# First attention: the key mask added by GpSimd to the shifted relative scores, in place of four mask products of TensorE a tile

## The chip, the core and the metric

The kernel runs on one core of a Trainium2 chip. Its engines work side by side and meet by semaphores: TensorE (PE, with its weight loads PEld), VectorE (DVE), ScalarE (ACT), GpSimd (POOL) and the Sync queue (SP), which here only issues transfers. The metric is the device time of one execution, in microseconds; less is better.

## The reference

Four blocks run one after another over 64 sequences of 64 tokens with 128 features. The change touches the first alone, a relative attention (16 heads of 64, 128 keys: 64 context tokens and the 64 own ones) with a feed-forward layer behind it.

```python
kv = concatenate([memory, layer_input], axis=1)            # 128 keys
ac = einsum('bqhd,bkhd->bhqk', q + content_bias, k)
bd = rel_shift(einsum('bqhd,khd->bhqk', q + position_bias, r))
scores = (ac + bd) * (1.0 / sqrt(d_head))
scores = where(slf_attn_mask[:, None, :, :], -1e9, scores) # mask: [64, 64, 128], one for all heads
attn = softmax(scores, axis=-1)
ctx = einsum('bhqk,bkhd->bqhd', attn, v)
out = layer_norm(layer_input + ctx @ Wo)                   # then the feed-forward layer
```

`rel_shift` moves row q of the relative scores by q places: it pads a column and reads the same memory with another row length.

## The kernel before

The first attention handles the 64 sequences in 32 tiles of two. A tile's 16 heads are worked on in 4 groups g; group g belongs to sequence b = g // 2 and holds 8 heads of it, two heads by 64 queries on the 128 partitions and four such pairs side by side (4 x 128 keys). Each engine has its own program, and `walk` runs the same `step` on all of them: `front` is the score part of tile m = n + 1, `back` the probability and output part of tile n, `head` the loading of tile n + 2. Inside the loop all three are on. The order on an engine is that in which its step is written, and the engines are held together only by the waits.

The work of a tile, with its lines:
- TensorE makes the relative scores of all heads (L1086, four groups of three matmuls, called in `step` for `l0_projected`). Group g takes the PSUM bank that the row maxima of group g of the tile before have read. VectorE adds a bias and keeps them in `rel_sb` (L612).
- The Sync queue first issues the loads of tile n + 2 (`load_tokens`: L324, L326, and the mask at L328), which wait for the last L1086 group, and then writes `rel_sb` to a scratch in memory (L346, two transfers). When they have landed it reads them back shifted into `rel_shifted` (L352, two transfers).
- TensorE makes the content products (L502, kept by ScalarE at L664), transposes the probabilities of the tile before (L494), and makes the scores in PSUM: for each group a mask product (L517: `twice` is the 64x64 identity twice side by side, and `mask_bias` the mask times -1e20 in bf16, so the product lays the mask on both heads) and four matmuls (L522) on top of it.
- VectorE adds `rel_shifted` to the scores and takes each head's row maxima (L634, 16 a tile), and negates and scales them after each sequence (L640). ScalarE takes the exponentials (L682, 16 a tile), VectorE normalises (L605).
- TensorE's context products (L532, kept at L674) and output products (L538) follow; VectorE adds them to `X` (L645) and takes statistics (L232, L236), from which GpSimd makes the inverse deviation (L241 to L245).
- GpSimd scales the mask (L408), copies the tokens (L417) and splits expert weights for a later block (L389, L392).

`wait_alone` is a wait with an empty instruction behind it.

Of the kernel before, what the change touches and what calls it, by code (L numbers as in the profile page):

```python
# [34 lines left out]
P = 128  # L35
# [76 lines left out]
def build(nc, a, out):  # L112
# [7 lines left out]
    with ctx:  # L120
        def sb(name, shape, dt=F32):
            return ctx.enter_context(nc.sbuf_tensor("sb_" + name, shape, dt))
# [3 lines left out]
        def sem(name):  # L126
            if name not in sems:
                sems[name] = ctx.enter_context(nc.semaphore("is_" + name))
            return sems[name]
# [3 lines left out]
        cols = sb("cols", [P, NCOLS])  # L133
        rows = sb("rows", [P, len(ROWS), D])
        ident = sb("ident", [P, P])
        twice = sb("twice", [S, P], BF16)
        token_mask = sb("token_mask", [P, NT])
        half_power = sb("half_power", [P, QT])
        next_stats = sb("next_stats", [P, QT, 6])
# [42 lines left out]
        def col(name):  # L182
            at, n = COLS[name]
            return cols[:, at:at + n]
# [105 lines left out]
        row_sum = carve((2, 2, 8))  # L290
        row_inv = carve((2, 2, 8))
        kv_in = sb("kv_in", [P, 2, 2, D])
        mask8 = ctx.enter_context(nc.sbuf_tensor("mask8", [S, 2, 2, KL], U8))
        mask_bias = ctx.enter_context(nc.sbuf_tensor("mask_bias", [S, 2, 2, KL], BF16))
        expert_halves = nc.dram_tensor("expert_halves", [2 * NE, P, 2 * FF], F32, kind="Internal").ap()
        expert_rows = nc.dram_tensor("expert_rows", [(NE + 1) * NTOK, ROW], F32, kind="Internal").ap()
        expert_outs = nc.dram_tensor("expert_outs", [2 * NTOK + GROUP, D], F32, kind="Internal").ap()
# [23 lines left out]
        def l0_sync(e, c):  # L321
            def load_tokens(u, m):

                e.dma_start(kv_in[0:S, u], ctx_in[bass.ds(2 * m, 2)].rearrange("b s d -> s b d"))\  # L324
                    .then_inc(sem(f"l0_kv_loaded{u}"), 16)
                e.dma_start(kv_in[S:P, u], x_in[bass.ds(2 * m, 2)].rearrange("b s d -> s b d"))\  # L326
                    .then_inc(sem(f"l0_kv_loaded{u}"), 16)
                e.dma_start(mask8[:, u], a["mask0"][bass.ds(2 * m, 2)].rearrange("b s k -> s b k"))\  # L328
                    .then_inc(sem(f"l0_mask_loaded{u}"), 16)

            for kind in ("rel", "qk", "vo"):
                for dst, src in l0_loads[kind]:
                    e.dma_start(dst, src).then_inc(sem(f"l0_{kind}_loaded"), 16)
            for u in range(2):
                load_tokens(u, u)
            for dst, src in loads:
                e.dma_start(dst, src).then_inc(sem("params_loaded"), 16)
            e.wait_ge(sem("params_loaded"), 16 * len(loads))
            meet(e, 0)

            def shift_relative(m):

                wait_alone(e, sem("l0_rel_kept"), kept_rel(m, 3) + 1)
                wait_alone(e, sem("l0_rel_read"), 32 * m)
                for b in range(2):
                    e.dma_start(scratch[b].rearrange("h (q c) -> q h c", q=S), rel_sb[S * b:S * b + S])\  # L346
                        .then_inc(sem("l0_rel_written"), 16)
                wait_alone(e, sem("l0_rel_written"), 32 * m + 32)
                wait_alone(e, sem("l0_rows_done"), 4 * m)
                for hh in range(2):  # L350
                    src = scratch[:, :, S:S + S * KL].rearrange("b (n two) (q k) -> two q (b n) k", two=2, q=S)
                    e.dma_start(rel_shifted[S * hh:S * hh + S].rearrange("p b n k -> p (b n) k"), src[hh])\  # L352
                        .then_inc(sem("l0_rel_read"), 16)

            def step(k, u, head, front, back):
                n = 2 * k + u
                m = n + 2
                if head and not opening(k):
                    wait_alone(e, sem("l0_kv_kept"), m - 1)
                    wait_alone(e, sem("l0_projected"), use_qk(m - 1, 0))  # L360
                    wait_alone(e, sem("l0_mask_ready"), m - 1)
                    load_tokens(u, m)
                if front:
                    shift_relative(n + 1)
            walk(e, NT, step)

        def l0_pool(e, c):
            e.memset(half_power[:, :], -0.5)
            e.memset(zeros[:, :], 0.0)
            e.wait_ge(sem("params_loaded"), 16 * len(loads))  # L370
            for i in range(2):
                e.tensor_copy(twice[:, S * i:S * i + S], ident[0:S, 0:S])
            e.tensor_copy(ident_16[:, :], ident[:, :])
            e.tensor_copy(bv_wide[:, 0], col("sa_bv").to_broadcast([P, P]))
            e.tensor_copy(bv_wide[:, 1], col("ca_bv").to_broadcast([P, P])).then_inc(sem("bv_wide"), 1)
            e.tensor_tensor(bases[:, 0], row("ln11_b"), row("ca1_bo"), ALU.add)
            meet(e, 0)
            e.memset(rel_sb[:, :, 0:1], 0.0).then_inc(sem("l0_rel_pad"), 1)
# [22 lines left out]
            def step(k, u, head, front, back):  # L401
                if back:
                    (store_expert if u else fetch_expert)(k)
                if head:
                    m = 2 * k + u + 2
                    e.wait_ge(sem(f"l0_mask_loaded{u}"), 16 * (k + 2))
                    wait_alone(e, sem("l0_rows_done"), 4 * (m - 1))
                    e.tensor_scalar(mask_bias[:, u], mask8[:, u], MASKED, None, ALU.mult)\  # L408
                        .then_inc(sem("l0_mask_ready"), 1)
                if back:  # L410
                    n = 2 * k + u
                    x_inv_std_pool(e, "l0", n + 1, n, 1)
                if head:
                    m = 2 * k + u + 2
                    wait_alone(e, sem(f"l0_kv_loaded{u}"), 32 * (k + 2))
                    wait_alone(e, sem("l0_context_done"), 8 * (m - 1))
                    e.tensor_copy(kv_tok[:, u], kv_in[:, u]).then_inc(sem("l0_kv_kept"), 1)  # L417
                if back and u:
                    wait_alone(e, sem("expert_stored"), 16 * k + 16)
                elif back:  # L420
                    split_expert(k)
            walk(e, NT, step)

        def l0_tensor(e, c):
# [22 lines left out]
            for left, right in ((wqT, wkT), (wqT, rT), (pb_wide, rT), (wvT, wo0)):  # L447
                if left is wvT:
                    e.wait_ge(sem("l0_vo_loaded"), 32)
                for q in range(4):  # L450
# [2 lines left out]
                        h = 4 * q + i  # L453
                        ins = e.matmul(o[:, i * P:(i + 1) * P], left[:, h], right[:, h], start=True, stop=True)
                    ins.then_inc(sem("l0_table_done"), 1)
            e.wait_ge(sem("bv_wide"), 1)
            for i, n in enumerate(("sa", "ca")):
                ins = e.matmul(PS[:, 2, P * i:P * i + P], bv_wide[:, i], w_out[n][:, :], start=True, stop=True)
            ins.then_inc(sem("bases_done"), 1)
            meet(e, 0)  # L460

            def step(k, u, head, front, back):
# [46 lines left out]
                    transpose_kv(k, u, n + 2)  # L509
                if front:  # L510
                    e.wait_ge(sem("l0_qk_kept"), 4 * m + 4)
                    e.wait_ge(sem("l0_mask_ready"), m + 1)
                    for g in range(4):
                        b = g // 2
                        o = PS[:, 4 + g]
                        e.wait_ge(sem("l0_rel_kept"), kept_rel(m, g) + 1)
                        e.matmul(o.rearrange("p (i k) -> p i k", i=4), twice[:, :],  # L517
                                 mask_bias[:, v, b].unsqueeze(1).to_broadcast([S, 4, KL]),
                                 start=True, stop=False, skip_group_check=True)
                        for i in range(4):  # L520
                            h = 8 * (g % 2) + 2 * i
                            ins = e.matmul(o[:, i * KL:i * KL + KL], qkT[:, b, h:h + 2],  # L522
                                           kvT[:, v, :, b], start=False, stop=(i == 3), skip_group_check=True)
                        ins.then_inc(sem("l0_scores_done"), 1)
                if back:
                    for g in range(2):
# [23 lines left out]
        def l0_vector(e, c):  # L550
# [11 lines left out]
            for table in ("QK", "QR", "rel_bias", "VO"):  # L562
                for q in range(4):
# [9 lines left out]
                        ins = e.tensor_copy(to[:, 4 * q:4 * q + 4], product)  # L573
                    ins.then_inc(sem("l0_table_drained"), 1)
                    n += 1
            e.wait_ge(sem("bases_done"), 1)
            for i, bias in enumerate(("sa_bo", "ca_bo")):
                e.tensor_tensor(bases[:, 1 + i], PS[:, 2, P * i:P * i + P], row(bias), ALU.add)
            meet(e, 0)
# [14 lines left out]
            def step(k, u, head, front, back):  # L594
# [30 lines left out]
                if head and not opening(k):  # L625
                    keep_kvT(n + 2, u)
                if front:
                    e.wait_ge(sem("l0_rel_read"), 32 * m + 32)
                    for g in range(4):
                        b = g // 2  # L630
                        wait_alone(e, sem("l0_scores_done"), 4 * m + g + 1)
                        for i in range(4):
                            hp = 4 * (g % 2) + i
                            ins = e.tensor_tensor_reduce(probs[:, v, b, hp], PS[:, 4 + g, i * KL:i * KL + KL],  # L634
                                                         rel_shifted[:, b, hp], 1.0, LOWEST, ALU.add, ALU.max,
                                                         row_max[:, v, b, hp:hp + 1])
                        ins.then_inc(sem("l0_rows_done"), 1)
                        if g % 2:
                            e.wait_ge(sem("l0_rows_done"), 4 * m + g + 1)
                            e.tensor_scalar(neg_max[:, v, b], row_max[:, v, b], -SCALE0, None, ALU.mult)\  # L640
                                .then_inc(sem("l0_max_ready"), 1)
# [1242 lines left out]
```

## Time and profile before

| | |
|---|---|
| median of 3 runs | 2367.7 us (2363.61 to 2370.63) |
| the profiled execution's own time | 2362.87 us |
| its span | 2361.0 us |
| first attention, first to last start of a tile's row maxima | 70.79 to 859.86 us |
| busy in that stretch: PE, DVE, ACT, POOL | 709.60, 421.38, 400.08, 140.65 us |
| mean granted TensorE clock in that stretch | 0.97 of full speed |

Times in the profile count from the span's start. A row of the timeline gives start, duration, engine, line, operation, destination and sources, how many instructions were merged, and in brackets how long the engine had been idle before and what it waited for. "SPq" is the Sync queue issuing a transfer, not the transfer's own time. A busy TensorE is not TensorE at its peak, since matmuls are pipelined. The busy share says little here: what counts is which wait ends last in a tile.

### The profile page before, as it was taken

What the parts mean: (1) busy time and instruction counts of PE and PEld (TensorE: products, weight loads), DVE (VectorE), ACT (ScalarE), POOL (GpSimd) and SP (SyncE); (2) the same over time, 40 slices, a digit from 0 to 9 for tenths busy, and PEclk for the clock granted to TensorE, in tenths of its full rate; (3) what the DMA queues carried; (4) which work ended last, traced back from release to release, by engine and by line L of the source; (5) the groups of instructions that cost most, each with busy time, mean ns of one, the idle gap of its engine ahead of it and who ended that gap; (6) DMA issues with size and microseconds to landing.
All of it is one profiled execution on the core that took longest, in us unless ns stands there. A gap on an engine that the chain in (4) does not pass through costs nothing. (4 is left out here: it accounts for less than half of the span.)

```text
span 2361.0 us, 53547 instructions
## 1 busy us (share of the span) xinstructions
PE 1858.5 (79%) x15946; PEld 1394.0 (59%) x15946; DVE 1403.0 (59%) x4243; ACT 1143.5 (48%) x3419; POOL 852.5 (36%) x1414
## 2 busy tenths in 40 slices
PE   8898998998999877799789977538997886225993
PEld 7666666766767656566566656215665664224772
DVE  3455555545545546487667764786774785224874
ACT  0455455445445543355456643216774774003772
POOL 0112112111112214355456653343442443443774
PEclk6899999999999998899899989668996997556997
DMA  6544444554454530222100000000000000004775
GB/s 167 106 95 108 106 97 96 113 107 97 108 107 90 117 69 0 104 91 92 60 14 16 16 6 0 0 0 1 0 0 11 12 11 10 27 27 129 224 216 168
DMA packets 214228, 166.54 MB, mean 71 GB/s; under 512 B 27216, under 2 KB 188368, under 8 KB 213776
## 3 DMA queue, kind: packets, MB, share of 16 engines
q1 hardware_dynamic: 205584, 142.84, 24.6%
q0 software_dynamic: 8576, 22.88, 2.8%
q8 instruction: 32, 0.52, 0.1%
q14 instruction: 36, 0.29, 0.0%
HBM read 91.92 MB, written 73.76 MB: 70 GB/s over the span
## 5 line engine op out<-in xcount | busy, mean ns | idle before, releaser
L241 POOL TENSOR_SCALAR sb_next_var_eps<-sb_next_moments 128x1 f32<-128x1 f32 (+1 forms) x184 | 43.2, 235 | 697.0 <-DVE sb_next_moments L236 695.8
L634 DVE CUSTOM_DVE_ANT_0 sb_probs<-PS,sb_work 128x128 f32<-128x128 f32 x512 | 113.3, 287 | 303.2 <-DMA sb_work<-rel_scratch 302.1
L788 POOL TENSOR_TENSOR sb_work<-sb_work,sb_cols 128x512 f32<-128x512 f32 x128 | 134.1, 1048 | 318.4 <-ACT sb_work L995 203.4
L682 ACT ACTIVATE sb_probs<-sb_probs,sb_work 128x128 f32<-128x128 f32 x512 | 197.8, 388 | 100.0 <-DVE sb_work L640 100.0
L926 DVE TENSOR_REDUCE sb_work<-PS 128x8 f32<-128x512 f32 x256 | 175.5, 686 | 87.1 <-PE PS L831 85.9
L674 ACT ACTIVATE sb_work<-PS 128x512 f32<-128x512 f32 x128 | 76.4, 597 | 291.5 <-PE PS L532 291.5
L502 PE MATMUL PS<-sb_work,sb_tables 128*128 128x128 f32 x1024 | 143.8, 298 | 64.1 <-ACT sb_work L664 64.1
L809 PE MATMUL PS<-sb_ident,sb_work 128*128 128x128 f32 x1024 | 168.3, 289 | 32.5 <-ACT sb_work L962 27.6
L962 ACT ACTIVATE sb_work<-sb_work 128x512 f32<-128x512 f32 x256 | 161.3, 630 | 59.9 <-DVE sb_work L928 59.2
L928 DVE TENSOR_TENSOR sb_work<-PS,sb_work 128x512 f32<-128x512 f32 x256 | 177.1, 692 | 8.8
L502 PEld LDWEIGHTS PS<-sb_work,sb_tables 128*128 128x128 f32 x1024 | 134.8, 206 | 74.2 <-ACT sb_work L664 70.2
L809 PEld LDWEIGHTS PS<-sb_ident,sb_work 128*128 128x128 f32 x1024 | 116.5, 145 | 69.1 <-ACT sb_work L962 54.5
L852 PE MATMUL PS<-sb_v_ones,sb_work 128*64 128x18 f32 x4096 | 147.3, 215 | 3.8 <-ACT sb_work L968 3.7
L522 PE MATMUL PS<-sb_work 128*128 128x128 f32 x1024 | 149.6, 290 | 0.0
L852 PEld LDWEIGHTS PS<-sb_v_ones,sb_work 128*64 128x64 f32 x4096 | 134.8, 142 | 22.4 <-issue 10.2
L664 ACT ACTIVATE sb_work<-PS,sb_key_bias 128x128 f32<-128x128 f32 x512 | 138.8, 366 | 17.8 <-PE PS L502 17.8
L968 ACT ACTIVATE sb_work<-PS 128x512 f32<-128x512 f32 x256 | 139.8, 595 | 6.1 <-PE PS L809 2.6
L522 PEld LDWEIGHTS PS<-sb_work 128*128 128x128 f32 x1024 | 125.1, 193 | 29.2 <-issue 29.2
L538 PEld LDWEIGHTS PS<-sb_tables,sb_work 128*128 128x128 f32 x1024 | 116.7, 192 | 21.0 <-ACT sb_work L674 21.0
L538 PE MATMUL PS<-sb_tables,sb_work 128*128 128x128 f32 x1024 | 122.5, 278 | 0.0
L245 POOL TENSOR_TENSOR sb_tile_inv_std<-sb_next_var_eps,sb_half_power 128x1 f32 (+3 forms) x184 | 119.0, 647 | 8.7
L623 DVE COPY sb_probsT<-PS 128x512 f32<-128x512 f32 x128 | 84.1, 688 | 61.4 <-PE PS L494 60.4
(272 smaller groups left out, 4357.4 us busy)
## 6 DMA issues: line engine op xcount, KB each, us to landing
rel_scratch<-sb_work SPq DMA_DIRECT2D x64, 516.0 KB, 6.5
sb_work<-rel_scratch SPq DMA_DIRECT2D x64, 512.0 KB, 6.5
expert_rows<-sb_blank SPq DMA_DIRECT2D x36, 520.0 KB, 2.8
sb_w_up<-expert_halves SPq DMA_DIRECT2D x23, 512.0 KB
sb_w_down<-expert_halves SPq DMA_DIRECT2D x23, 512.0 KB
expert_halves<-sb_e_halves POOLq DMA_DIRECT2D x16, 512.0 KB, 8.2
sb_work<-expert_rows SPq DMA_DIRECT2D x23, 260.0 KB
sb_e_raw<-e_W POOLq DMA_DIRECT2D x16, 256.0 KB, 3.0
```

Of the source, the lines that this page charges most:

```text
L502: ins = e.matmul(PS[:, (shift + g) % 2, i * P:i * P + P], QK[:, 4 * g + i], kvT[:, v, 1], start=True, stop=True)
L522: ins = e.matmul(o[:, i * KL:i * KL + KL], qkT[:, b, h:h + 2], kvT[:, v, :, b], start=False, stop=(i == 3), skip_group_check=True)
L538: ins = e.matmul(o[:, 0:D], pkvT[:, h], VO[:, h], start=(h == 0), stop=(h == H - 1))
L664: ins = e.activation(qkT[:, :, h], PS[:, (shift + g) % 2, i * P:i * P + P] .rearrange("p (b q) -> p b q", b=2), ACT.Identity, bias=key_bia ...
L682: ins = e.activation(probs[:, v, b, hp], probs[:, v, b, hp], ACT.Exp, bias=neg_max[:, v, b, hp:hp + 1], scale=SCALE0, accum_out=row_sum[:, ...
L788: e.tensor_tensor(k_masked[:, u], k_sb[:, u].rearrange("p (b k) -> p b k", b=2).unsqueeze(2) .to_broadcast([P, 2, 4, S]), col("place").uns ...
L809: ins = e.transpose(PS[:, 4 + j, i * P:i * P + P], att_probs[:, u, 8 * j + 2 * i:8 * j + 2 * i + 2], ident[:, :])
L852: ins = e.matmul(values[S * b:S * b + S, 2 * i:2 * i + 2], att_probsT[:, i, S * b:S * b + S], v_ones[:, u, b, 2 * i:2 * i + 2], start=True ...
L926: e.tensor_reduce(top, mine, AX.X, ALU.max).then_inc(sem("att_max_ready"), 1)
L928: e.tensor_tensor(by_group(att_probs[:, v])[:, 2 * j:2 * j + 2], mine, top.unsqueeze(3).to_broadcast([P, 2, 4, S]), ALU.subtract)\
L962: e.activation(att_probs[:, v, 8 * j:8 * j + 8], att_probs[:, v, 8 * j:8 * j + 8], ACT.Exp, scale=c["scale"]).then_inc(sem("att_exp_done"), 1)
L968: e.activation(att_probsT[:, 4 * j:4 * j + 4].rearrange("p i q -> p (i q)"), PS[:, 4 + j], ACT.Copy)\
```

## The change

The mask is no longer a product. It is scaled to f32 on all 128 partitions (both head halves, so it is loaded twice), and GpSimd adds it to `rel_shifted` once the shifted scores have been read back: one add of 128 x 1024 for each of the two sequences. VectorE's row maxima wait for these adds (`l0_rel_masked`) where they waited for the transfer (`l0_rel_read`). TensorE's scores are only the four matmuls a group. `twice` goes, and two semaphores become one.

```diff
-        mask8 = ctx.enter_context(nc.sbuf_tensor("mask8", [S, 2, 2, KL], U8))
-        mask_bias = ctx.enter_context(nc.sbuf_tensor("mask_bias", [S, 2, 2, KL], BF16))
+        mask8 = ctx.enter_context(nc.sbuf_tensor("mask8", [P, 2, 2, KL], U8))
+        mask_bias = ctx.enter_context(nc.sbuf_tensor("mask_bias", [P, 2, 2, KL], F32))
...
-                e.dma_start(mask8[:, u], a["mask0"][bass.ds(2 * m, 2)].rearrange("b s k -> s b k"))\
-                    .then_inc(sem(f"l0_mask_loaded{u}"), 16)
+                for hh in range(2):
+                    e.dma_start(mask8[S * hh:S * hh + S, u], a["mask0"][bass.ds(2 * m, 2)].rearrange("b s k -> s b k"))\
+                        .then_inc(sem(f"l0_mask_loaded{u}"), 16)
...
-            for i in range(2):
-                e.tensor_copy(twice[:, S * i:S * i + S], ident[0:S, 0:S])
...
-                    e.wait_ge(sem(f"l0_mask_loaded{u}"), 16 * (k + 2))
-                    wait_alone(e, sem("l0_rows_done"), 4 * (m - 1))
+                    e.wait_ge(sem(f"l0_mask_loaded{u}"), 32 * (k + 2))
+                    wait_alone(e, sem("l0_rel_masked"), 2 * (m - 1))
                     e.tensor_scalar(mask_bias[:, u], mask8[:, u], MASKED, None, ALU.mult)\
                         .then_inc(sem("l0_mask_ready"), 1)
+                if front:
+                    m, v = 2 * k + u + 1, 1 - u
+                    wait_alone(e, sem("l0_rel_read"), 32 * m + 32)
+                    wait_alone(e, sem("l0_mask_ready"), m + 1)
+                    for b in range(2):
+                        e.tensor_tensor(rel_shifted[:, b], rel_shifted[:, b],
+                                        mask_bias[:, v, b].unsqueeze(1).to_broadcast([P, 8, KL]), ALU.add)\
+                            .then_inc(sem("l0_rel_masked"), 1)
...
-                    e.wait_ge(sem("l0_mask_ready"), m + 1)
                     for g in range(4):
                         b = g // 2
                         o = PS[:, 4 + g]
                         e.wait_ge(sem("l0_rel_kept"), kept_rel(m, g) + 1)
-                        e.matmul(o.rearrange("p (i k) -> p i k", i=4), twice[:, :],
-                                 mask_bias[:, v, b].unsqueeze(1).to_broadcast([S, 4, KL]),
-                                 start=True, stop=False, skip_group_check=True)
                         for i in range(4):
                             h = 8 * (g % 2) + 2 * i
                             ins = e.matmul(o[:, i * KL:i * KL + KL], qkT[:, b, h:h + 2],
-                                           kvT[:, v, :, b], start=False, stop=(i == 3), skip_group_check=True)
+                                           kvT[:, v, :, b], start=True, stop=True)
...
                 if front:
-                    e.wait_ge(sem("l0_rel_read"), 32 * m + 32)
                     for g in range(4):
                         b = g // 2
+                        if g % 2 == 0:
+                            wait_alone(e, sem("l0_rel_masked"), 2 * m + b + 1)
                         wait_alone(e, sem("l0_scores_done"), 4 * m + g + 1)
```

On GpSimd, this is the start of the loop's first step before (`sb_work` is the area in which `rel_shifted`, `rel_sb` and the token copies lie):

```order
L384 DMA sb_e_raw<-e_W 128x512
L406 ISA
L71 ISA [waits is_l0_mask_loaded0]
L408 TENSOR_SCALAR mask_bias<-mask 64x256 [waits is_l0_rows_done]
L241 TENSOR_SCALAR sb_next_var_eps<-sb_next_moments 128x1 [waits is_x_moments]
```

and the same place after:

```order
L382 DMA sb_e_raw<-e_W 128x512
L404 ISA
L71 ISA [waits is_l0_mask_loaded0]
L406 TENSOR_SCALAR mask_bias<-mask 128x256 [waits is_l0_rel_masked]
L71 ISA
L71 REGISTER_ALU [waits is_l0_rel_read]
L413 TENSOR_TENSOR sb_work<-sb_work,mask_bias 128x1024 [waits is_l0_mask_ready]
L413 TENSOR_TENSOR sb_work<-sb_work,mask_bias 128x1024
L240 TENSOR_SCALAR sb_next_var_eps<-sb_next_moments 128x1 [waits is_x_moments]
```

The two adds stand between the mask's scaling and the statistics, and wait for the transfer that VectorE waited for.

On the Sync queue, the loop's first step before:

```order
L71 ISA [waits is_l0_kv_kept]
L324 ISA [waits is_l0_projected,is_l0_mask_ready]
L324 DMA sb_kv_in<-ctx 64x2x128
L326 DMA sb_kv_in<-x 64x2x128
L328 DMA mask<-mask 64x2x128
L71 ISA
L71 REGISTER_ALU [waits is_l0_rel_kept]
L346 DMA rel_scratch<-sb_work 64x16x129 [waits is_l0_rel_read]
```

and after:

```order
L71 ISA [waits is_l0_kv_kept]
L323 ISA [waits is_l0_projected,is_l0_mask_ready]
L323 DMA sb_kv_in<-ctx 64x2x128
L325 DMA sb_kv_in<-x 64x2x128
L328 DMA mask<-mask 64x2x128 x2
L71 ISA
L71 REGISTER_ALU [waits is_l0_rel_kept]
L346 DMA rel_scratch<-sb_work 64x16x129 [waits is_l0_rel_read]
```

One more load stands ahead of the scratch write; nothing else of the queue's order is changed.

## Rows read from the trace of the kernel before

**Rows 1.** The waits from 60 to 870 us: total us, times, longest.
```profile
DVE sb_probs L634 <- DMA sb_work<-rel_scratch: 302.1, 32, 16.6
```

**Rows 2.** Timeline: the first row maxima of the first and of the last tile.
```profile
70.79 0.29 DVE L634 CUSTOM_DVE_ANT_0 sb_probs<-PS,sb_work 128x128 f32<-128x128 f32 x1 [16.61 <-DMA sb_work<-rel_scratch]
...
859.86 0.29 DVE L634 CUSTOM_DVE_ANT_0 sb_probs<-PS,sb_work 128x128 f32<-128x128 f32 x1 [9.99 <-DMA sb_work<-rel_scratch]
```

**Rows 3.** Timeline: the round from 427.51 us.
```profile
427.51 0.29 DVE L634 CUSTOM_DVE_ANT_0 sb_probs<-PS,sb_work 128x128 f32<-128x128 f32 x1 [10.17 <-DMA sb_work<-rel_scratch]
...
429.52 0.29 DVE L634 CUSTOM_DVE_ANT_0 sb_probs<-PS,sb_work 128x128 f32<-128x128 f32 x1
...
431.33 0.17 DVE L640 TENSOR_SCALAR sb_work<-sb_work 128x8 f32<-128x8 f32 x1
...
431.91 0.39 PE L1086 MATMUL PS<-sb_QR_parts,sb_own_lo 128*128 128x512 f32 x1
...
432.61 0.63 SPq L324 DMA_DIRECT2D sb_kv_in<-ctx  x1
...
432.93 2.49 DVE L612 TENSOR_TENSOR sb_work<-PS,sb_rel_bias 128x512 f32<-128x512 f32 x4 [0.43 <-issue]
...
435.62 1.32 SPq L346 DMA_DIRECT2D rel_scratch<-sb_work  x2
...
443.97 1.31 SPq L352 DMA_DIRECT2D sb_work<-rel_scratch  x2
...
452.21 0.29 DVE L634 CUSTOM_DVE_ANT_0 sb_probs<-PS,sb_work 128x128 f32<-128x128 f32 x1 [7.65 <-DMA sb_work<-rel_scratch]
```

**Rows 4.** Timeline: the round from 401.69 us.
```profile
401.11 3.83 PE L538 MATMUL PS<-sb_tables,sb_work 128*128 128x128 f32 x32
...
401.69 0.29 DVE L634 CUSTOM_DVE_ANT_0 sb_probs<-PS,sb_work 128x128 f32<-128x128 f32 x1 [8.17 <-DMA sb_work<-rel_scratch]
...
408.14 0.63 SPq L324 DMA_DIRECT2D sb_kv_in<-ctx  x1
...
410.54 1.32 SPq L346 DMA_DIRECT2D rel_scratch<-sb_work  x2
...
419.26 1.31 SPq L352 DMA_DIRECT2D sb_work<-rel_scratch  x2
```

**Rows 5.** GpSimd's groups: count, then busy us, mean ns of one; and one mask scaling.
```profile
L788 POOL TENSOR_TENSOR sb_work<-sb_work,sb_cols 128x512 f32<-128x512 f32 x128 | 134.1, 1048 | 318.4 <-ACT sb_work L995 203.4 <-ACT sb_work L997 115.0
...
L1080 POOL TENSOR_TENSOR sb_qT_lo<-sb_work,sb_qT_hi 128x512 fp32r<-128x512 f32 x16 | 20.7, 1292 | 37.3 <-ACT sb_qT_hi L1074 37.3
...
L782 POOL TENSOR_TENSOR sb_X<-sb_work,sb_rows 128x128 f32<-128x128 f32 x4 | 1.8, 456 | 0.3
...
436.35 1.15 POOL L408 TENSOR_SCALAR mask_bias<-mask 64x256 bf16<-64x256 uint8 x1 [1.38 <-DMA mask<-mask]
```

**Rows 6.** Timeline: GpSimd beside VectorE, 406 to 413 us.
```profile
406.70 2.48 DVE L612 TENSOR_TENSOR sb_work<-PS,sb_rel_bias 128x512 f32<-128x512 f32 x4
...
408.16 1.03 POOL L389 TENSOR_TENSOR sb_e_halves<-sb_e_raw,sb_zeros 128x512 fp32r<-128x512 f32 x1
...
409.34 2.34 POOL L392 TENSOR_TENSOR sb_e_halves<-sb_e_raw,sb_e_halves 128x512 fp32r<-128x512 f32 x1
...
410.70 2.07 DVE L605 TENSOR_TENSOR sb_probs<-sb_probs,sb_work 128x1024 f32<-128x1024 f32 x1
```

**Rows 7.** Windows, TensorE (us, busy, PEclk, DMA), and the timeline of the first round.
```profile
70.79:74.20 3.41, 2.42 (x6) 0.50 0.01 2
...
71.78 0.80 PE L1086 MATMUL PS<-sb_QR_parts,sb_own_hi 128*128 128x512 f32 x1 [4.20 <-DVE sb_work L634]
...
74.88 0.17 DVE L640 TENSOR_SCALAR sb_work<-sb_work 128x8 f32<-128x8 f32 x1
...
77.09 0.65 SPq L324 DMA_DIRECT2D sb_kv_in<-ctx  x1
```

**Rows 8.** The group of mask products, from 0 to 950 us.
```profile
L517 PE MATMUL PS<-mask_bias,sb_twice 64*128 64x512 bf16 x128 | 49.6, 388 | 1.2 <-ACT sb_work L664 1.2
```

More of the change, by code:

```diff
@@ L135, in build @@
         ident = sb("ident", [P, P])
-        twice = sb("twice", [S, P], BF16)
         token_mask = sb("token_mask", [P, NT])
@@ L370, in l0_pool @@
             e.wait_ge(sem("params_loaded"), 16 * len(loads))
-            for i in range(2):
-                e.tensor_copy(twice[:, S * i:S * i + S], ident[0:S, 0:S])
             e.tensor_copy(ident_16[:, :], ident[:, :])
             e.tensor_copy(bv_wide[:, 0], col("sa_bv").to_broadcast([P, P]))
-            e.tensor_copy(bv_wide[:, 1], col("ca_bv").to_broadcast([P, P])).then_inc(sem("bv_wide"), 1)
+            e.tensor_copy(bv_wide[:, 1], col("ca_bv").to_broadcast([P, P])).then_inc(sem("bases"), 1)
             e.tensor_tensor(bases[:, 0], row("ln11_b"), row("ca1_bo"), ALU.add)
@@ L455, in l0_tensor @@
                     ins.then_inc(sem("l0_table_done"), 1)
-            e.wait_ge(sem("bv_wide"), 1)
+            e.wait_ge(sem("bases"), 1)
             for i, n in enumerate(("sa", "ca")):
                 ins = e.matmul(PS[:, 2, P * i:P * i + P], bv_wide[:, i], w_out[n][:, :], start=True, stop=True)
-            ins.then_inc(sem("bases_done"), 1)
+            ins.then_inc(sem("bases"), 1)
             meet(e, 0)
@@ L575, in l0_vector @@
                     n += 1
-            e.wait_ge(sem("bases_done"), 1)
+            e.wait_ge(sem("bases"), 2)
             for i, bias in enumerate(("sa_bo", "ca_bo")):
```

## The prediction

> **What bounds the kernel now.** I read the waits of the first attention first, since only that stage is edited. In [rows 1] VectorE's row maxima (L634) wait for the read of the shifted scores in all 32 tiles, 302.1 us, 9.4 us a tile. The stage therefore runs in a loop of its own: read lands, row maxima, relative scores of the next tile, write, read. From the first read to the last [rows 2] it does 31 rounds in 859.86 - 70.79 = 789.07 us, 25.45 us each.
>
> Next I took two neighbouring rounds apart in the timeline. In the round that starts at 427.51 [rows 3] the second row maxima's negation (L640, end of the 16 maxima) starts at +3.82. TensorE's last L1086 group, which needs the last maxima's bank, ends at +4.79, the Sync queue starts its token loads (L324) at +5.10, VectorE ends the four relative scores (L612, 2.49 us from 432.93) at +7.91, the write (L346) starts at +8.11, the read (L352) 8.35 later, and the next maxima 8.24 after that. In the round from 401.69 [rows 4] TensorE is late instead: L538 of the tile before runs until 404.94 (+3.25), so L324 starts at +6.45, and three load issues later the write starts at +8.85. Here the Sync queue is last, for L612 was done at 409.18 (406.70 + 2.48, [rows 6]). The two rounds are 25.82 and 24.70 us. What matters for the change: every us between landing and write counts once a tile, and TensorE's work counts only by the 0.7 us that it holds L324 back in every other tile.
>
> **What is removed.** Four mask products a tile, 0.388 us each, 49.6 us in all [rows 8]. They run while the scratch write and read are in flight, between the key transposes and L522. Removing them makes L538 end about 1.55 us earlier in its tile, which is worth the lateness of [rows 4] and nothing else: no more than 0.74 us every other tile. The two casts to `twice` in the prologue lie beside TensorE's table products and are costed at nothing (both ends: 0 to 0.5 us once).
>
> **What is added on the path.** The adds start where the maxima started: at the landing. I call one add A: 128x1024, both inputs f32 in SBUF, one repeated over eight heads. No such row exists. The nearest: 128x512 with two full inputs takes 1.292 us, 128x128 takes 0.456 us, 128x512 with a narrow second input 1.048 us [rows 5]. The slope from 128 to 512 is (1292 - 456)/384 = 2.18 ns an element, so 1024 elements give 1.292 + 512 x 0.00218 = 2.41 us. The bounds are 2 x 1.048 = 2.10 us and 2 x 1.292 = 2.58 us. I take 2.35, a little under the slope, because L1080 also rounds its output. The two adds are serial on GpSimd, and VectorE follows half by half. The first half's maxima (about 2.0 us) hide under the second add; then the second half's maxima are bare. The second negation starts at 2A + 0.05 (an estimate for the gap between two GpSimd instructions; between L389 and L392, where the second waits for the first, it is 0.15 in [rows 6]) + 0.20 (hand-over, taken from that of L612's end at 435.42 to the write at 435.62) + 1.81 (431.33 - 429.52) = 6.76, where it was 3.82: +2.94 us.
>
> **What is added on the Sync queue.** One more mask load in front of each write. In [rows 4] three loads and the start of the write take 410.54 - 408.14 = 2.40 us, so a load is between 0.63 (L324's own issue) and 0.80 (a third of it); I take 0.73, and four take 3.13. L324 comes 5.10 - 3.82 = 1.28 after the second negation, as now in the clean round, because the later maxima give TensorE time to finish L538. So the write starts at 6.76 + 1.28 + 3.13 = 11.17. VectorE's own branch (L612) is done at 6.76 + 4.09 = 10.85, which would let the write start at 11.05: the fourth load makes the Sync queue last by 0.12 us. The write-to-read time is taken as 8.72, that of the round in which loads directly precede the write, and 8.25 from read to maxima. Round: 11.17 + 8.72 + 8.25 = 28.14 us; 31 rounds 872.3 against 789.07: **+83.3 us**. The last tile has no round behind it, but its exponentials also start later, by A + 0.20: +2.5.
>
> **What is moved without cost.** The mask's scaling now fills 128 partitions at the same 256 elements a partition; it ran in 1.15 us at 436.35 [rows 5], 15 us ahead of the landing at 452.21. If that cover were gone it would cost its 1.1 us a tile. The adds stand in GpSimd's order ahead of the statistics (L241 to L245) and the token copy (L417), which wait for VectorE's moments behind the maxima anyway. The rest of the tile (exponentials, transposes, L532, L538) starts A + 0.20 = 2.55 us later in a round that is 28.14 - 25.45 = 2.7 us longer, and sheds the 1.55 us of the mask products: L538, whose latest end in the two rounds is +3.25, would end at about +1.6 or before. TensorE's first L1086 must wait for four maxima, which took 71.78 - 70.79 = 0.99 us, and so for 2.55 + 0.99 = +3.5: there is room, and TensorE isn't late in any round.
>
> **The clock.** TensorE now stands still before L1086, from L538's end to +3.5. The trace shows once what this does: at 71.78, after 4.20 us of idling, L1086's matmuls take 0.80 us, not 0.39 (the granted clock was 0.50 of full speed in this stretch, its lower level, 1.2 GHz), and L324 comes 77.09 - 74.88 = 2.21 us after the second negation, not 1.28 [rows 7]. That is +0.93 us on the path of a tile in which the clock has fallen. The idle stretch, from L538's end (+1.6 at the latest, and by my estimate up to 2 us before) to +3.5, will be 2 to 4 us; I take half the tiles: 31 x 0.5 x 0.93 = **+14 us** (bounds 0 and 29).
>
> **Sum.** 83.3 + 2.5 + 14 = +100 us on the profiled execution's own 2362.87 us: 2463. The median of the runs shown lies 4.8 us above that execution, within their spread of 7 us; I leave the number at 2463.
>
> **A rule against the trace.** In [rows 6] GpSimd and VectorE block each other: L392 takes 2.34 us beside L605, where L1080 takes 1.292 us for the same size and inputs [rows 5], and L605 takes 2.07 us; but L389 takes 1.03 us, no more than L788's 1.048 of the same kind, beside L612, which reads PSUM and one SBUF tensor and keeps a pace of 0.62 us. The row maxima read the same kinds of operands as L612, so I count no blocking. The Trainium skill, "SBUF — State Buffer", section "Who interferes with whom", says that a VectorE instruction with at most one SBUF input, outside the two-port modes, doesn't contend with GpSimd, while one with two SBUF inputs does; by that rule the trace agrees, and the sum stays. The Trainium skill's "GPSIMD Engine Reference", section 3.1, gives 4497 ns for an f32 add of 2048 elements; halved, as an estimate, A would be 2.25 us and the sum 6 us less; no row here has that size.
>
> **Rivals.**
> Blocking after all: if the maxima can't run beside an add, VectorE gets nothing until the second add ends, and all 16 maxima are bare: 4.75 + 0.20 + 3.82 = 8.77 in place of 6.76, +2.0 us a tile, 62 us: about 2525. For it: L605 beside L392. Against: L612 beside L389. Chance 0.09.
> A cheaper add and a clock that stays up: A = 2.10 takes 0.5 us from each round and no tile pays the clock: 2463 - 15 - 14 = 2434, or a few us less if Sync's issue shrinks. Chance 0.06, for what lies below 2432.
> Faster: TensorE's relief pays. If TensorE's chain ended last in a tile, up to the 49.6 us of [rows 8] would come back: 2313. It decides only if VectorE, at the maxima, waits for TensorE; in the trace it waits for the transfer 32 times in 32, and the adds sit behind that same transfer. Chance 0.03, and 0.02 for no change.
> My forecast: 0.80.
>
> **How the numbers follow.** The range of my case goes from A = 2.10 without a clock loss (2434) to A = 2.58 (2 x 0.23 x 31 = +14) with every tile paying the clock (+15): 2492, and a little for hand-overs: 2432 to 2496. It leaves out the blocking case, the cheaper tail, the faster one and no change: 0.09 + 0.06 + 0.03 + 0.02 = 0.20. A measurement of this kernel tells 0.3% (7 us) from no change; the cases give faster 0.03, same 0.02, slower 0.95.
>
> **What would show it.** Adds of 2.3 to 2.4 us on GpSimd, the first starting at the landing; the maxima waiting for GpSimd 32 times, and in the middle a second time; negation to negation 2.2 to 2.4 us; the first token load 1.3 us behind the second negation or 2.2 with a low clock; four loads and then the write with no gap; rounds near 28 to 29 us; the other stages unchanged. It would be wrong if the adds overlap less (blocking, maxima longer than 0.21 us apart), if A is outside 2.1 to 2.6, or if another wait, such as TensorE's chain at half clock, becomes the round.

## The result, and the profile after

The changed kernel takes 2477.47 us (median of 4 runs, 2474.02 to 2482.41) where the kernel before took 2368.05: a ratio of 1.0464, with a 95% interval of 1.0443 to 1.0485. It is 4.6% slower. 2463 us had been forecast, with a range of 2432 to 2496. On another chip the same pair later gave 1.0517 (1.0491 to 1.0544).

The profiled execution took 2474.27 us, 111.4 more than that of before. First the page's costliest groups and the waits from 60 to 980 us (total us, times, longest), the answers to [rows 1] and [rows 5]:

```profile
L637 DVE CUSTOM_DVE_ANT_0 sb_probs<-PS,sb_work 128x128 f32<-128x128 f32 x512 | 113.2, 287 | 427.9 <-POOL sb_work L413 427.9
L413 POOL TENSOR_TENSOR sb_work<-sb_work,mask_bias 128x1024 f32<-128x1024 f32 x64 | 149.0, 2347 | 458.3 <-DMA sb_work<-rel_scratch 458.3
...
L1089 PE MATMUL PS<-sb_QR_parts,sb_own_hi 128*128 128x512 f32 x256 | 122.7, 573 | 151.9 <-DVE sb_work L637 151.0
```
```profile
POOL sb_work L413 <- DMA sb_work<-rel_scratch: 458.3, 32, 21.7
DVE sb_probs L637 <- POOL sb_work L413: 427.9, 64, 19.4
```

The transfer is now waited for by GpSimd, and VectorE waits for GpSimd twice a tile. One add takes 2.347 us. The relative products (L1089, L1086 before) have become slower without any change to them.

Then a round in the timeline, from 446.90 us (the answer to [rows 3]; L637 are the row maxima, L643 the negation, L614 the relative scores, L323 to L328 the loads, L346 the write, L352 the read):

```profile
446.90 4.65 POOL L413 TENSOR_TENSOR sb_work<-sb_work,mask_bias 128x1024 f32<-128x1024 f32 x2 [14.28 <-DMA sb_work<-rel_scratch]
449.52 0.29 DVE L637 CUSTOM_DVE_ANT_0 sb_probs<-PS,sb_work 128x128 f32<-128x128 f32 x1 [13.50 <-POOL sb_work L413]
449.74 0.28 DVE L637 CUSTOM_DVE_ANT_0 sb_probs<-PS,sb_work 128x128 f32<-128x128 f32 x1
...
450.60 1.19 PE L1089 MATMUL PS<-sb_QR_parts,sb_own_hi 128*128 128x512 f32 x2 [5.23 <-DVE sb_work L637]
...
451.84 0.29 DVE L637 CUSTOM_DVE_ANT_0 sb_probs<-PS,sb_work 128x128 f32<-128x128 f32 x1 [0.26 <-POOL sb_work L413]
...
453.65 0.17 DVE L643 TENSOR_SCALAR sb_work<-sb_work 128x8 f32<-128x8 f32 x1
...
454.83 2.48 DVE L614 TENSOR_TENSOR sb_work<-PS,sb_rel_bias 128x512 f32<-128x512 f32 x4
...
455.24 0.63 SPq L323 DMA_DIRECT2D sb_kv_in<-ctx  x1
...
456.69 1.29 SPq L328 DMA_DIRECT2D mask<-mask  x2
...
458.30 1.32 SPq L346 DMA_DIRECT2D rel_scratch<-sb_work  x2
...
467.14 1.31 SPq L352 DMA_DIRECT2D sb_work<-rel_scratch  x2
...
475.58 4.66 POOL L413 TENSOR_TENSOR sb_work<-sb_work,mask_bias 128x1024 f32<-128x1024 f32 x2 [13.35 <-DMA sb_work<-rel_scratch]
```

The reader should see four things. The second negation stands 453.65 - 446.90 = 6.75 us after the landing (3.82 in [rows 3]). The row maxima run 0.21 us apart beside the second add, as before: nothing blocks. TensorE stood idle for 5.23 us, and its first two products then take 1.19 us together (the granted clock is 0.50 of full speed from 450.60 to 453.30); over the stage such a product takes 0.573 us on average, where it took 0.433 in the kernel before. The write follows the loads at once, 3.06 us after L323, while L614 had ended at 457.31.

Nearly the whole loss lies in this stage. The first and the last landing:

```profile
68.54 4.65 POOL L413 TENSOR_TENSOR sb_work<-sb_work,mask_bias 128x1024 f32<-128x1024 f32 x2 [21.66 <-DMA sb_work<-rel_scratch]
...
968.71 4.63 POOL L413 TENSOR_TENSOR sb_work<-sb_work,mask_bias 128x1024 f32<-128x1024 f32 x2 [17.64 <-DMA sb_work<-rel_scratch]
```

31 rounds take 900.17 us, 29.04 each, where they took 789.07: +111.1 of the 111.4 us. The first landing came 2.3 us earlier and what lies behind the last one took 2.5 us longer, so the rest cancels here. In the second pair of profiles (experiments 6 and 7) the 31 rounds take 117.3 of 124.1 us more; the other 7 lie behind the stage, and why was not looked into.

### The profile page after: what moved, and what is told of

Same layout as the page of the kernel before. It is cut to its first block and busy times, and to the rows that moved or that the text cites. A ratio compares the mean times of both kernels' runs of the same rounds, so it can differ in the third digit from the quotient of the medians.

```text
span 2472.3 us, 53543 instructions
## 1 busy us (share of the span) xinstructions
PE 1829.4 (74%) x15818; PEld 1398.7 (57%) x15818; DVE 1404.1 (57%) x4243; ACT 1144.7 (46%) x3419; POOL 998.0 (40%) x1476
## 5 line engine op out<-in xcount | busy, mean ns | idle before, releaser
L637 DVE CUSTOM_DVE_ANT_0 sb_probs<-PS,sb_work 128x128 f32<-128x128 f32 x512 | 113.2, 287 | 427.9 <-POOL sb_work L413 427.9
L413 POOL TENSOR_TENSOR sb_work<-sb_work,mask_bias 128x1024 f32<-128x1024 f32 x64 | 149.0, 2347 | 458.3 <-DMA sb_work<-rel_scratch 458.3
L1089 PE MATMUL PS<-sb_QR_parts,sb_own_hi 128*128 128x512 f32 x256 | 122.7, 573 | 151.9 <-DVE sb_work L637 151.0
L1089 PEld LDWEIGHTS PS<-sb_QR_parts,sb_own_hi 128*128 128x128 f32 x256 | 66.6, 282 | 180.7 <-DVE sb_work L637 84.4
L540 PEld LDWEIGHTS PS<-sb_tables,sb_work 128*128 128x128 f32 x1024 | 116.7, 192 | 21.0 <-ACT sb_work L677 21.0
L540 PE MATMUL PS<-sb_tables,sb_work 128*128 128x128 f32 x1024 | 122.6, 278 | 0.0
```

The costliest lines, as they stand in the source:

```text
L413: e.tensor_tensor(rel_shifted[:, b], rel_shifted[:, b], mask_bias[:, v, b].unsqueeze(1).to_broadcast([P, 8, KL]), ALU.add)\
L540: ins = e.matmul(o[:, 0:D], pkvT[:, h], VO[:, h], start=(h == 0), stop=(h == H - 1))
L1089: ins = e.matmul(o, left[l], right[r], start=(i == 0), stop=(i == 2))
```

## The experiments

Twelve runs were made, two of them of unchanged kernels, in three groups, each group on one chip beside the kernel before. The chips differ: it took 2365.9, 2377.5 and 2369.6 us in the three. So ratios are compared, and the parts of a round within a group where it has both kernels. The changed kernel itself ran beside the kernel before only in the first result (1.0464) and in the third group (1.0517), so a ratio of the other groups is held against a number that differs by 0.5% between these two.

**1. The adds left out.** From the changed kernel:

```diff
-                    for b in range(2):
-                        e.tensor_tensor(rel_shifted[:, b], rel_shifted[:, b], ...)
...
                 if front:
+                    e.wait_ge(sem("l0_rel_read"), 32 * m + 32)
                     for g in range(4):
-                        if g % 2 == 0:
-                            wait_alone(e, sem("l0_rel_masked"), 2 * m + b + 1)
```

> Leaves out the mask: the changed kernel without GpSimd's adds, VectorE's row maxima waiting for the transfer again; doubled mask load and missing mask products stay. Theory (the adds on the path cost nearly all): the second negation comes back from 6.75 to 3.82 us after the landing, the rounds from 29.0 to 25.3 to 26.1 us, the time to 2360 to 2385. Rival (the cost is mostly elsewhere: the fourth load, TensorE's clock, the transfers): 2400 or more.

Measured 2367.21 us, ratio 0.9997 (0.9985 to 1.001). VectorE waits for the transfer again:

```profile
DVE sb_probs L628 <- DMA sb_work<-rel_scratch: 293.3, 32, 17.2
```

The whole 4.6% goes with the adds, what they do to the clock included: without them the second negation stands at 3.83 us, the token loads 1.34 us behind it, and a round takes 25.42 us (means over rounds 3 to 29). The doubled load and the missing products together are worth nothing that can be measured. The rival is out.

**2. Half the heads.** `rel_shifted[:, b, 0:4]` in place of `rel_shifted[:, b]`, and the mask repeated over 4.

> Masks only four of each sequence's eight heads: two adds of 128x512 in place of 128x1024. Theory: an add is now 1.29 us, shorter than the eight row maxima (2.0 us), so the second add hides completely and the second negation stands at 1.29 + 0.25 + 3.82 = 5.36 us after the landing: 1.39 us less a round, about 2434. Rival (the maxima can't run beside an add): both adds stay bare, 2 x 1.05 = 2.1 us less a round, about 2412.

Measured 2435.85 us, ratio 1.0293 (1.0258 to 1.0328). One round:

```profile
456.46 2.49 POOL L413 TENSOR_TENSOR sb_work<-sb_work,mask_bias 128x512 f32<-128x512 f32 x2 [12.83 <-DMA sb_work<-rel_scratch]
458.02 0.29 DVE L637 CUSTOM_DVE_ANT_0 sb_probs<-PS,sb_work 128x128 f32<-128x128 f32 x1 [10.06 <-POOL sb_work L413]
...
459.83 0.17 DVE L643 TENSOR_SCALAR sb_work<-sb_work 128x8 f32<-128x8 f32 x1
...
460.18 0.29 DVE L637 CUSTOM_DVE_ANT_0 sb_probs<-PS,sb_work 128x128 f32<-128x128 f32 x1 [0.18 <-issue]
...
462.00 0.17 DVE L643 TENSOR_SCALAR sb_work<-sb_work 128x8 f32<-128x8 f32 x1
```

The second add ends at 458.95, in the middle of the first eight maxima, and the second eight wait for nothing but their own queue. The second negation stands at 5.54 us (5.36 expected; the first hand-over is longer, 458.02 - 456.46 less 1.26 for an add = 0.30). The time is the theory's, 2434, not the rival's 2412. The trace is the stronger evidence of the two, for the time has a second part: the token loads stand 1.63 us behind the negation on average, where it is 2.04 in the changed kernel, and that is worth another 0.4 us a round.

**3. The adds on VectorE.** The same two instructions, each ahead of its sequence's maxima in `l0_vector`, with a wait on their own semaphore behind each.

> The same two f32 adds, on VectorE ahead of each sequence's row maxima. Theory (what counts is the bare time between landing and second negation): 2 x 1.22 (VectorE's own 128x1024 two-input instruction) + 3.82 + about 0.2 of hand-overs = 6.5 against 6.75 us: some 8 us less, 2465 to 2475. Rival (GpSimd's part costs more than its instructions show, by hand-overs): 30 us less or more.

Measured 2468.26 us, ratio 1.0422 (1.0393 to 1.045).

```profile
L627 DVE TENSOR_TENSOR sb_work<-sb_work,mask_bias 128x1024 f32<-128x1024 f32 x63 | 77.0, 1222 | 358.2 <-DMA sb_work<-rel_scratch 358.2
```

An add takes 1.222 us here, about half of GpSimd's 2.347, and still the second negation stands at 6.73 us, as late as with GpSimd's 6.76: on GpSimd one of the adds overlaps the maxima, on VectorE none does. The negation had been expected at 6.5 us; behind each of the two adds VectorE waits 0.29 us, 0.58 in all where 0.2 had been counted. So that the time fell within the expected 2465 to 2475 does not bear the sum out: 0.03 us a round came from the negation, where the expected 8 us need 0.25. Against 1.0464 nothing is gained that the intervals would show; the changed kernel was not in this group, and against its other ratio, 1.0517, it would be 1%. This stays unclear. That hand-overs on GpSimd cost 30 us is not borne out: the negation moved by 0.03 us.

**4. and 5. TensorE kept busy.** From the changed kernel, ahead of the relative products (40, and in a second kernel 18):

```diff
                     e.wait_ge(sem("l0_own_split"), m + 1)
+                    if not opening(k):
+                        for i in range(40):
+                            e.matmul(PS[:, i % 2, 0:P], QK[:, i % H], ident[:, :], start=True, stop=True)
```

> The changed kernel with 40 more 128x128 matmuls (4.8 us at full clock, into free banks, results unused) ahead of each tile's relative products, where TensorE stands idle for 5.2 us. Theory (the fallen clock is on the path through the last relative product): the token loads start 1.3 us after the second negation in every round, not 1.95 on average: 0.65 x 31 = 20 us less, about 2457. Rival (the clock is off the path): 2477, unchanged; more if the matmuls hold the relative products up.

Measured 2514.94 us, ratio 1.0613 (1.059 to 1.0636). I had the size wrong: each of these f32 matmuls stands as two instructions in the trace, and the 40 take 9.10 us where 4.8 had been counted.

```profile
462.18 9.10 PE L479 MATMUL PS<-sb_ident,sb_tables 128*128 128x128 f32 x80
471.03 0.71 PE L1092 MATMUL PS<-sb_QR_parts,sb_own_hi 128*128 128x512 f32 x2
```

They held up the relative products, which then ran at full clock (1.00 from 471.00 to 474.00) but too late. This decided nothing on the clock, so it was made again with 18, and with both kernels unchanged beside it.

> The changed kernel with 18 unused f32 matmuls (36 passes, 4.1 us) ahead of each tile's relative products, in place of 40 (9.1 us), which held them up. They end before the first row maxima free a bank (5.2 us after the products of the tile before). Theory (the fallen clock is on the path): the granted clock stays near 1.00, the loads start 1.3 us after the second negation in every round, and the time falls by 0.67 us a round, 20 us: ratio to the kernel before about 1.038. Rival (the clock is off the path): 1.046, unchanged.

Measured 2466.63 us, ratio 1.0398 (1.0376 to 1.042), where the changed kernel unchanged had 1.0517 on this chip: 26.4 us less (2493.02 - 2466.63), where 20 were expected. From 100 to 840 us the granted clock was 0.89 and 0.96 of full speed, first the changed kernel, then the one with 18 (columns: us, then busy us and instructions of PE, PEld, DVE, ACT and POOL, PEclk, DMA share, GB/s):

```profile
100.00:840.00 740.00, 558.93 (x3352) 453.12 (x3353) 344.35 (x1315) 321.82 (x1300) 232.88 (x228) 0.89 0.43 90
```
```profile
100.00:840.00 740.00, 651.72 (x4367) 544.37 (x4367) 356.27 (x1352) 336.51 (x1352) 238.87 (x234) 0.96 0.44 93
```

**6. and 7. Both kernels unchanged on that chip.**

> The kernel before, unchanged, profiled in the same job as the next three, for the parts of a round on one chip. If the 8.6 us from write to read of its first profile is a matter of the chip, it may move here by some 0.3 us; the time ratio is 1.

> The changed kernel, unchanged, on the same chip. Theory (all of the excess over the forecast is the clock): write to read is the same as in the kernel before here, and the token loads start 1.6 to 2.3 us after the second negation. Rival (the doubled mask load also lengthens the transfers behind it): write to read 0.2 us above that of the kernel before on this chip, 6 us in all.

Measured 2370.89 and 2493.02 us, ratios 1.0 (0.9987 to 1.0014) and 1.0517. The parts of a round, worked out from the timelines of the four profiles of this group and the two first ones, as means over rounds 3 to 29, in us. The first three columns count from the landing.

| kernel | second negation | token loads | write | write to read | read to landing | round |
|---|---|---|---|---|---|---|
| before, first profile | 3.83 | 5.92 | 8.61 | 8.60 | 8.30 | 25.51 |
| after, first profile | 6.76 | 8.80 | 11.86 | 8.84 | 8.37 | 29.06 |
| before again | 3.83 | 5.70 | 8.28 | 9.08 | 8.31 | 25.67 |
| after again | 6.76 | 8.95 | 12.00 | 9.09 | 8.37 | 29.46 |
| with 18 matmuls | 6.78 | 8.09 | 11.14 | 9.05 | 8.41 | 28.60 |
| relative scores first (experiment 9) | 3.85 | early | 7.21 | 9.18 | 8.45 | 24.84 |

Write to read is 9.08 and 9.09 on one chip: the doubled mask load isn't seen to lengthen the transfers there, so the rival of 0.2 us is out on this chip. The first two profiles differ by 0.24 us; whether both were taken on one chip is not on record, and the cause of that difference stays open. From negation to token loads there are 2.19 us in the changed kernel and 1.31 with the 18 matmuls: 0.88 us a round, 27 us in 31 rounds, against the 26.4 measured. That is the price of the fallen clock on this chip. The products themselves show it: L1089's first kind took 0.602 us on average from 60 to 980 us in the changed kernel, and 0.442 with the 18 matmuls ahead of them.

**8. The parts in the kernel before.** The second load alone (`for hh in range(2)` around the mask's transfer), and the mask products alone taken out.

> The kernel before with the mask loaded twice, as after the change (the second copy unused). Theory (a load issue in front of the write costs 0.73 us where the Sync queue is last, and 0.12 in the rounds in which VectorE is): 0.43 us a round, 13 us, about 2381. Rival (it is hidden): 2368. Rival (the extra small packets hold the write up too): 2390 or more, with write to read above 8.9 us.

Measured 2391.52 us, ratio 1.0075 (1.0053 to 1.0097): 18 us by the ratio, 14 by the medians (2391.52 - 2377.49), where 13 were expected; the six runs spread over 24 us. By its number this meets the second rival (2390 or more, write to read above 8.9), for write to read is 9.05 us. But it is 9.07 on this chip without the second load too (`before_no_product`), so the transfers are not what the load lengthened. What moved is the write: it stands 8.62 us after the landing.

> Leaves out the mask: the kernel before without the four mask products a tile. Theory: worth only TensorE's lateness in every other round, about 0.37 us a round, 11 us less: 2357. Rival (TensorE's chain carries weight): up to 49.6 us less, 2320. Rival (the freed time lets the clock fall more often): 2368 or more.

Measured 2368.71 us, ratio 0.9966 (0.9953 to 0.9979): 8 us less where 11 were expected. TensorE's 49.6 us of products are worth 8. The two ratios together would leave 0.4%, and the first experiment, which has both parts, left nothing (0.9997, 0.9985 to 1.001); the times don't settle that difference. The place of the write does add up: 8.28 us in "before again", 8.62 with the second load, 7.96 without the products, 8.23 with both, all means over rounds 3 to 29, though on three chips, and the kernel before had 8.61 in its first profile.

**9. Loads earlier, and relative scores first.** In `l0_sync`, for both kernels:

```diff
-                    wait_alone(e, sem("l0_projected"), use_qk(m - 1, 0))
+                    wait_alone(e, sem("l0_projected"), 9 * n + 1)
```

`9 * n + 1` counts up to the key transposes of tile n, whose buffer the loads overwrite, where before it counted up to the last relative product of tile n + 1. The loads are then issued right behind the read (L352) of the step before.

> The changed kernel with the same earlier loads. Theory (fourth load and fallen clock act only through the load issues in front of the write): the write comes 0.2 us after VectorE's relative scores, 10.8 us after the landing where it was 11.8 on average: 0.95 us a round, 29 us less, about 2448. Rival (only the fourth load is on the path, not the clock): 0.12 to 0.4 us a round, 2465 to 2474.

Measured 2459.16 us, ratio 1.0347 (1.0333 to 1.0361). The changed kernel wasn't in this group; against its 1.0464 and 1.0517 in the others that is 28 and 40 us less, where 29 were expected, and well outside the rival's 3 to 12. The write came 10.85 us after the landing on average, 0.2 us behind VectorE's relative scores (10.64). With the loads out of the way the last product has time: it ends at 8.64, and VectorE takes up that group's scores only some 0.7 us before 10.64. The granted clock is still low (0.91 from 100 to 840 us), and it costs nothing any more: it acted only through the load issues.

> The kernel before, with the token and mask loads waiting only for what they overwrite (the transposes of the tile two before) and no longer for the last relative product, so that they are issued while the shifted scores are being read. Theory: VectorE's relative scores alone set the write, at 7.7 to 8.1 us after the landing where it was 8.5 on average: 0.6 us a round, 19 us less, about 2349. Rival (the loads then collide with the read of the shifted scores): 2368 or more, with read to maxima above 8.6 us.

Measured 2367.06 us, ratio 0.9964 (0.9951 to 0.9977): faster, by 9 to 10 us where 19 were expected. The write came at 7.92 us as expected, but I had counted from 8.5, the first profile's; where the transfers are slower TensorE is less often late, and "before again" in the table has its write at 8.28 with nothing changed. There is a price as well, smaller than the rival had it: with the loads beside the read, read to landing is 8.44 us (8.47 in the changed kernel with early loads), where the table has 8.31 and 8.37 without.

The last kernel also moves VectorE's relative scores of the next tile (L612) from the head of the next step to right behind the row maxima:

```diff
+                if front and head:
+                    keep_relative(m + 1)
                 if back:
                     e.wait_ge(sem("l0_out_done"), n + 1)
```

> The kernel before, with the earlier loads, and with VectorE keeping the next tile's relative scores right behind the row maxima, ahead of the residual add and its statistics. Theory (every us between landing and write counts once a tile, and these 1.2 us do no work for the write): the relative scores are kept 2.7 us after the second negation where it was 3.7 to 4.1, the write at 6.7 us after the landing where it was 8.5: up to 1.9 us a round, 59 us, less what TensorE's late output products take back: 2310 to 2335, ratio 0.975 to 0.987. Rival (TensorE's chain takes its place as the bound at once): 0.99 or more, with the last relative product ending as late as before.

Measured 2346.5 us, ratio 0.9891 (0.9864 to 0.9918): faster than both kernels, but outside the expected 0.975 to 0.987, by the mechanism of the rival. In 12 of the 31 rounds TensorE takes over, and the write stands 0.7 to 2.3 us behind its best place, 6.71 us:

```profile
444.98 2.79 DVE L612 TENSOR_TENSOR sb_work<-PS,sb_rel_bias 128x512 f32<-128x512 f32 x4 [0.88 <-PE PS L1090]
...
446.64 0.39 PE L1090 MATMUL PS<-sb_QR_parts,sb_own_lo 128*128 128x512 f32 x1
...
447.68 0.28 DVE L649 TENSOR_TENSOR sb_X<-sb_X,PS 128x128 f32 x1
447.96 1.32 SPq L346 DMA_DIRECT2D rel_scratch<-sb_work  x2
```

This round landed at 440.10. VectorE waits 0.88 us for the products, whose last ends at 447.03, +6.93, later than in the round of [rows 4], where it was +6.03. The next round (465.44) has its last product at +4.83 and its write at +6.74, the expected place. The 31 rounds of this profile are 28.0 us shorter than in "before again" (768.6 and 796.6 us), but what lies behind them took 12.9 us longer (1515.4 and 1502.5); why is open. In the fourteen profiles that part takes from 1501.1 to 1515.4 us, so that a whole time can be off by some us for reasons outside the stage.

## Why the prediction was right

**The bound.** The stage is a chain from landing to landing, and what is put on it counts once a tile. Right: 111.1 of 111.4 us are in its 31 rounds, and without the adds the ratio is 0.9997.

**The adds.** A = 2.35 was forecast and 2.347 measured; the estimate with the Trainium skill's figure had been 2.25, and the rows' own slope 2.41. The step down from the slope was a judgement, and its reason (that L1080 also rounds) was not tested. The second negation was forecast at 6.76 us and stands at 6.76. Some of that exactness is luck: the two adds take 4.65 us where 4.75 was counted, and the hand-over 0.29 (451.84 - 451.55) where 0.20 was. The middle wait is there, 0.26 us.

**No blocking.** Right: maxima 0.21 us apart beside an add, and half an add hides whole (experiment 2). By that trace the rule in the Trainium skill, "SBUF — State Buffer", "Who interferes with whom", held for this custom instruction too, with one SBUF and one PSUM input. The rival of 2525 us is out; so is the one of TensorE's relief, which is worth 8 us where 49.6 would have been its most.

**The fourth load.** Right in kind: the write stands 3.06 us behind the first load (3.13 forecast), against 2.69 on average with three. Taken alone it costs 14 to 18 us in the kernel before.

**The clock.** The mechanism was right, and the size too small. I gave half the tiles 0.93 us and the others nothing. In the first profile 8.80 - 6.76 = 2.04 us lie between negation and token loads, 0.76 above the 1.28 of a clean round, where 0.47 was forecast: 9 us more in 31 rounds. The term that was off is the share and the price of the tiles. Of rounds 3 to 29, 14 pay 1.11 us on average, which is the forecast's half, a little dearer; but the other 13 pay 0.39, which had been taken as nothing. In the round shown the gap is 1.59 us, in the next one 2.34.

The idle stretch had been taken as 2 to 4 us. It is 5.23 in the round shown (L540, the L538 of before, ended 1.53 us before the landing there, 441.54 + 3.83 = 445.37) and 3.3 to 6.3, 4.6 on average, in rounds 3 to 29. But its length is not what sets the price of a round. The next round has the shorter stretch and pays more:

```profile
479.19 0.73 PE L1089 MATMUL PS<-sb_QR_parts,sb_own_hi 128*128 128x512 f32 x2 [3.28 <-DVE sb_work L637]
...
481.51 1.22 PE L1089 MATMUL PS<-sb_QR_parts,sb_own_hi 128*128 128x512 f32 x2 [0.41 <-DVE sb_work L637]
```

The granted clock is 1.00 from 479.20 to 480.70 and 0.50 from 480.80 to 484.10: it falls after TensorE has taken up work again, and then the last products are the slow ones, which the token loads wait for. In the round shown it was low from the first product and back at 1.00 from 453.50, before the last. The forecast knew only a clock that is low when the products begin. With the 18 matmuls the write stands at 11.14, the forecast's 11.17 for a clock that stays up.

**The sum.** Forecast round 28.14 + 0.47 = 28.61, measured 29.04. Of the 0.43 missing, 0.29 is the clock, 0.12 write to read and 0.12 read to landing (8.84 and 8.37 for 8.72 and 8.25), less 0.07 for the loads; that is 0.46, from means over slightly different rounds. The two transfer times were taken from a single round, and such a time varies between rounds (write to read 8.38 to 9.51 in rounds 3 to 29) and between profiles of the same kernel (8.60 and 9.08). That read to landing is 0.06 us longer in both changed profiles was not looked into.

## What to carry to other kernels

In a loop held together by a transfer there and back, ask of each instruction only whether it lies between landing and next write. TensorE's four products lay beside the transfer and cost 8 us for 49.6 busy; GpSimd's adds lay on the chain and cost 4.6%. Here VectorE made an add in half the time, and the negation came no earlier, since the overlap was lost. And look at what stands in the queue ahead of the instruction that closes the loop: loads that wait for something they don't need, and residual adds ahead of the work that the next transfer waits for, were worth 1.1% here with no work removed.

## What had not been expected of the hardware

An engine off the chain got slower when it stood idle more, and this reached the chain. TensorE's granted clock from 100 to 840 us fell from 0.97 (before again) to 0.89 of full speed, the two levels being 1.2 and 2.4 GHz, once it stood idle some 5 us a tile; 18 useless matmuls a tile brought it back to 0.96 and made the whole kernel 26.4 us faster. And write to read took 8.60 us in one profile of the kernel before and 9.08 in another, with the same code. Within each group it hardly changes with the kernel (8.73 to 8.89, 9.05 to 9.08 and 9.05 to 9.18 us). So the chip is the likely cause, but no run shows it: the chip of the 8.60 is not on record.
